# Expert picks of a vision tower's expert layer: one-hot products and sums moved to GpSimd, packing deferred by one tile

## What is computed

```python
q = (hidden_states @ w_queries.T).reshape(b, t, 2, h, n)
sim = jnp.einsum('btphn,hkpn->pbthk', q, keys)
sx, ix = jax.lax.top_k(sim[0], k)
sy, iy = jax.lax.top_k(sim[1], k)
all_scores = (sx[..., :, None] + sy[..., None, :]).reshape(b, t, h, k * k)
all_idx = (ix[..., :, None] * nk + iy[..., None, :]).reshape(b, t, h, k * k)
scores, pos = jax.lax.top_k(all_scores, k)
indices = jnp.take_along_axis(all_idx, pos, axis=-1)
de = down_embed[indices]
ue = up_embed[indices]
ew = jnp.einsum('btd,bthkd->bthk', hidden_states, de)
ew = jax.nn.silu(ew) * jax.nn.softmax(scores, axis=-1)
experts_states = jnp.einsum('bthk,bthkd->btd', ew, ue)
mlp = jax.nn.silu(hidden_states @ w_gate.T) * (hidden_states @ w_up.T) @ w_down.T
return mlp + experts_states
```

## Time and profile before

| | us |
|---|---|
| median of 3 runs (lowest, highest) | 275.31 (274.69, 276.77) |
| profiled execution, its time | 276.26 |
| profiled execution, span of the core | 274.5 |
| TensorE busy | 246.7 (90%) |
| VectorE busy | 181.0 (66%) |
| ScalarE busy | 56.9 (21%) |
| GpSimd busy | 47.7 (17%) |
| chain that ended last | TensorE 50%, VectorE 40% of the span |

### The profile page before, as it was taken

One profiled execution on the slowest core, in us unless ns is written; L12 is line 12 of the kernel. 1 busy time (PEld: TensorE's weight loads), 2 busy tenths in 40 slices (PEclk: granted clock), 3 DMA queues, 4 the chain that ended last, 5 costly groups with the idle time before them and its releaser, 6 DMA issues.

```text
span 274.5 us, 4828 instructions
## 1 busy us (share of the span) xinstructions
PE 246.7 (90%) x1956; PEld 204.2 (74%) x1956; DVE 181.0 (66%) x461; ACT 56.9 (21%) x104; POOL 47.7 (17%) x65
## 2 busy tenths in 40 slices
PE   3998975788865999899999989899979999999996
PEld 2675654677642588889898989888868888888763
DVE  0047298888885139999999999799968767511100
ACT  1101136343453142213131743100000000000000
POOL 5023155001112523224052630000000000000000
PEclk9999999999965699999999999999999999999999
DMA  7960000221003252053115330300000000000000
GB/s 256 383 229 0 2 0 0 89 73 32 19 20 93 58 184 73 0 171 99 39 45 188 111 121 1 88 2 2 0 19 2 0 19 2 0 19 2 19 0 12
DMA packets 14805, 16.99 MB, mean 62 GB/s; under 512 B 848, under 2 KB 12992, under 8 KB 14784
## 3 DMA queue, kind: packets, MB, share of 16 engines
q1 hardware_dynamic: 13776, 15.70, 17.6%
q10 hardware_dynamic: 1008, 1.00, 1.1%
HBM read 15.48 MB, written 1.21 MB: 61 GB/s over the span
## 4 chain that ended last, share of the span: by engine, by line
PE 50%; DVE 40%; issue 3%; ACT 2%; DMA 1%; POOL 1%; DVEq 0%; ACTq 0%
PE ps L1053 20%; PE ps L1016 9%; PE ps L808 7%; PE ps L1075 4%; DVE big L783 4%; DVE topi L684 3%; DVE late L669 3%; PE ps L972 3%; DVE top L681 3%; DVE big L533 2%; PE ps L1050 2%; DVE red L575 2%; DVE big L577 2%; PE ps L835 2%; DVE slots L665 2%
## 5 line engine op out<-in xcount | busy, mean ns | idle before, releaser
L1053 PE MATMUL ps<-ue,big 128*128 128x256 f32 (+1 forms) x320 | 72.3, 381 | 1.4 <-DVE big L783 1.4
L1053 PEld LDWEIGHTS ps<-ue,big 128*128 128x128 f32 (+1 forms) x320 | 57.2, 182 | 12.1 <-DVE big L783 1.8
L1016 PE MATMUL ps<-hn_hi,de_hi 128*128 128x296 f32 x128 | 40.7, 318 | 2.1 <-ACT big L468 1.1
L783 DVE TENSOR_TENSOR big<-ps,big 128x1024 f32<-128x1024 f32 (+1 forms) x19 | 22.7, 1197 | 26.9 <-PE ps L1075 26.2
L1016 PE MATMUL ps<-hn_lo,de_hi 128*128 128x296 f32 x128 | 38.3, 300 | 0.0
L1016 PE MATMUL ps<-hn_hi,de_lo 128*128 128x296 f32 x128 | 38.2, 298 | 0.0
L468 ACT ACTIVATE big<-ps 128x592 f32<-128x592 f32 x32 | 21.1, 666 | 44.5 <-PE ps L1016 44.4
L1016 PEld LDWEIGHTS ps<-hn_hi,de_hi 128*128 128x128 f32 x128 | 24.1, 188 | 4.5 <-DVE actT L730 1.9
L1016 PEld LDWEIGHTS ps<-hn_lo,de_hi 128*128 128x128 f32 x128 | 24.1, 188 | 1.2 <-issue 1.2
L1016 PEld LDWEIGHTS ps<-hn_hi,de_lo 128*128 128x128 f32 x128 | 24.1, 188 | 0.0
L669 DVE TENSOR_TENSOR late<-eqx,wsel 128x2048 f16<-128x2048 f16 (+1 forms) x19 | 22.7, 1197 | 0.7
(11 more groups left out here) (113 smaller groups left out, 337.6 us busy)
## 6 DMA issues: line engine op xcount, KB each, us to landing
de<-in_down_t SPq DMA_DIRECT2D x16, 256.0 KB, 2.8
ue<-in_up_e SPq DMA_DIRECT2D x4, 1024.0 KB, 5.7
big<-in_patches SPq DMA_DIRECT2D x6, 296.0 KB, 5.0
big<-in_w_tok ACTq DMA_DIRECT2D x6, 128.0 KB, 5.3
big<-in_w_qkv SPq DMA_DIRECT2D x1, 768.0 KB, 8.4
h_scratch<-big SPq DMA_DIRECT2D x5, 111.0 KB
late<-in_keys_bd SPq DMA_DIRECT2D x1, 512.0 KB, 9.7
downT<-in_wdown_t SPq DMA_DIRECT2D x1, 512.0 KB, 9.3
```

The lines of the kernel that those rows point to most:

```text
L783: chain(nc.vector.tensor_tensor(dst, pv, dst, ALU.mult), g_ready)
L1016: last = mm(ps[:, 2 + 2 * (e % 2) + a, 0:HALF], half[:, (e // 2) % SPLITS, k, own], src[:, k, a * HALF:(a + 1) * HALF], start=(n == 0), st ...
L1053: last = mm(acc, sil[:, e, j * 128:j * 128 + Q * v], ue[:, e, :], start=False, stop=(e == EX - 1))
```

## The change

VectorE still makes the one-hots of both sides, now into one buffer `oneh` of 128 x 2 x 256 that lies in `xn`, and gives `oneh_ready`. The product with `topf` and the sum over eight, now as three halvings, are done by GpSimd for both sides at once (`picks`). The picks of tile 0 to 3 stand ahead of splits 8, 10, 12 and 14, those of tile 4 behind split 15. `topf` and `pick` have two buffers. The one-hots of tile j wait for the picks of tile j - 1 (`picked`), and the clamp and packing of tile j - 1 (`packed`) stand behind the one-hots of tile j; those of the last tile stand ahead of the denominators.

```diff
+PICK_FROM = 8
...
-        topf = sb("topf", [128, 2, FH, TOPK])
+        topf = sb("topf", [128, 2, 2, FH, TOPK])
...
-        pick = sb("pick", [128, 2, FH, TOPK])
-        oneh = sb("oneh", [128, FH, TOPK, TOPK])
+        pick = sb("pick", [128, 2, 2, FH, TOPK])
...
+        oneh = xn[:, :, :].rearrange("p a (h k c) -> p a h k c", h=FH, k=TOPK)
...
+            def picks(j):
+
+                pool.wait_ge(oneh_ready, 2 * (j + 1))
+                nc.gpsimd.tensor_tensor(oneh[:, :, :, :, :], oneh[:, :, :, :, :],
+                                        topf[:, j % 2].unsqueeze(3).broadcast_to([128, 2, FH, TOPK, TOPK]),
+                                        ALU.mult).then_inc(pick_chain, 1)
+                pool.wait_ge(pick_chain, 3 * j + 1)
+                nc.gpsimd.tensor_tensor(oneh[:, :, :, :, 0:4], oneh[:, :, :, :, 0:4], oneh[:, :, :, :, 4:8],
+                                        ALU.add).then_inc(pick_chain, 1)
+                pool.wait_ge(pick_chain, 3 * j + 2)
+                nc.gpsimd.tensor_tensor(oneh[:, :, :, :, 0:2], oneh[:, :, :, :, 0:2], oneh[:, :, :, :, 2:4],
+                                        ALU.add).then_inc(pick_chain, 1)
+                pool.wait_ge(pick_chain, 3 * j + 3)
+                nc.gpsimd.tensor_tensor(pick[:, j % 2], oneh[:, :, :, :, 0], oneh[:, :, :, :, 1],
+                                        ALU.add).then_inc(picked, 1)
+
             for i in range(EX // 2):
+                if i >= PICK_FROM and (i - PICK_FROM) % 2 == 0:
+                    picks((i - PICK_FROM) // 2)
...
+            picks(TILES - 1)
...
+            def packed(j):
+
+                at = pick[:, j % 2]
+                behind()
+                chain(nc.vector.tensor_scalar(over[:, :, :], at[:, 0], float(EX), float(NK - 1), ALU.is_ge, ALU.mult))
+                chain(nc.vector.tensor_scalar(pack[:, j, 0, :].rearrange("p (h k) -> p h k", h=FH), at[:, 0],
+                                              float(EX - 1), None, ALU.min))
+                behind()
+                chain(nc.vector.tensor_tensor(pack[:, j, 1, :].rearrange("p (h k) -> p h k", h=FH), at[:, 1],
+                                              over[:, :, :], ALU.max))
+
...
                 chain(nc.vector.tensor_copy(self_[:, :, :, :], sel[:, :, :, :]))
+                behind()
+                if j >= 1:
+                    dve.wait_ge(picked, j)
                 for p in range(2):
-                    behind()
-                    chain(nc.vector.tensor_tensor(oneh[:, :, :, :],
-                                                  self_[:, p].unsqueeze(3).broadcast_to([128, FH, TOPK, TOPK]),
+                    chain(nc.vector.tensor_tensor(oneh[:, p], self_[:, p].unsqueeze(3).broadcast_to([128, FH, TOPK, TOPK]),
                                                   iota8.unsqueeze(1).unsqueeze(1).broadcast_to([128, FH, TOPK, TOPK]),
-                                                  ALU.is_equal))
-                    behind()
-                    chain(nc.vector.tensor_tensor(oneh[:, :, :, :], oneh[:, :, :, :],
-                                                  topf[:, p].unsqueeze(2).broadcast_to([128, FH, TOPK, TOPK]),
-                                                  ALU.mult))
-                    behind()
-                    chain(nc.vector.tensor_reduce(pick[:, p], oneh[:, :, :, :], AX.X, ALU.add))
...
+                                                  ALU.is_equal), oneh_ready)
+                if j >= 1:
+                    packed(j - 1)
...
+            dve.wait_ge(picked, TILES)
+            packed(TILES - 1)
             dve.wait_ge(lg_exp, 1)
```

More of the change, by code:

```diff
@@ L250, in vit_tower @@
         split_ready = sem("split_ready")
+        oneh_ready, picked, pick_chain = sem("oneh_ready"), sem("picked"), sem("pick_chain")
         pe_s, sil_ready = sem("pe_s"), sem("sil_ready")
@@ L686, in _ @@
                 behind()
-                chain(nc.vector.tensor_copy(topf[:, :, :, :], topi[:, :, :, :]))
+                chain(nc.vector.tensor_copy(topf[:, j % 2], topi[:, :, :, :]))
                 chain(nc.vector.tensor_tensor(cand[:, :, :, :],
```

## The result

The changed kernel takes 282.69 us (median of 4 runs, 282.12 to 283.3), the kernel before 275.66 beside it; the ratio is 1.0258, with a 95% interval of 1.0221 to 1.0296. It is 7.0 us slower; 283.4 us in all and 8.1 us more had been predicted.

What follows compares the result with a forecast made beforehand. VectorE was taken to set the rounds of 11.87 us, with TensorE alone needing 11.64. Rounds 1.4, last tile 5.6 and clock 1.1 made 8.1 us on the median of 275.3: 283.4 us, range 279.2 to 288.

Steps and rivals of the forecast that it cites:

- The place in the queue: On GpSimd, picks stand behind splits 7, 9, 11, 13, 15, which TensorE holds back, so VectorE waits for them.
- The cost of the picks: Four GpSimd operations per tile, sized by a straight line between two trace rows, with hand-overs: 3.2 us.
- The rounds: Rounds of 12.63 us instead of 11.87, as VectorE's comparison waits for GpSimd's picks; 1.4 us later after three.
- P: Length of one tile's picks on GpSimd, set at 3.2 us, with bounds of 2.42 and 4.8.
- X: Moment in a round when TensorE's odd expert, the second after a gated block, may start, once `actT` frees its banks.
- A sign that came out otherwise: Expected in the profile after: VectorE idle about 2.5 us before the comparison of tiles 1 to 4, released by GpSimd.
- The last tile: Last picks wait for split 15, so VectorE's packing starts 6.85 us later, 1.22 of it idle now: 5.6 us.
- X3: The odd expert's start on TensorE three rounds after the first: 147.46 us before the change, forecast at 148.87.
- The clock: TensorE idles 4.7 us before the first product, its clock falls, and two later rounds no longer fit: 1.1 us.
- The sum: Whole kernel: +1.4 + 5.6 + 1.1 = 8.1 us on the median of 275.3, giving 283.4 us.
- the rival on the other side: Last tile's picks ready in time and not waited for, rounds at TensorE's 11.64 us: faster, 273.8 us; chance 0.04.

Runs made afterwards that it cites:

- both_early: Changed kernel with picks of tiles 0 to 3 ahead of splits 7, 9, 11, 13 and the last tile's ahead of split 14; 277.13 us, ratio 1.006.
- gap_filled: Changed kernel with 28 matmuls that nobody reads added in TensorE's gap behind the second round of slots; 280.68 us, ratio 1.0222.
- load_without_waits: Kernel before, picks still on VectorE, plus the same four operations per tile on GpSimd over scratch, not waited for until long done; 282.57 us.
- longer_picks: Changed kernel with one more product of 128x512 into scratch in each tile's picks on GpSimd; 289.4 us, ratio 1.0534.
- last_on_dve_mid_early: Changed kernel with picks of tiles 0 to 3 one split earlier and the last tile's products and sums back on VectorE; 276.1 us, ratio 1.0038.
- mid_early: Changed kernel with only the picks of tiles 0 to 3 moved one split earlier, the last ones staying behind split 15; 280.57 us, ratio 1.0179.

## Why the prediction was right

**The place in the queue.** It said that VectorE would wait behind splits 7, 9, 11, 13 and 15. It does, at each of the five places, and moving the picks out from behind them takes back 6.3 of 6.65 us in the profiled execution of both_early, 2.0 of 2.6% in whole runs.

**The cost of the picks.** 3.2 us were set, 2.94 to 2.98 measured: 1.28, 0.73, 0.40 and 0.30 us and three hand-overs. The straight line between the earlier trace rows gave 1.29, 0.76, 0.49 and 0.36; the small ones were set too high, and rows of four, two and one neighbouring elements cost nothing above the line. The slope between the two largest is 2.15 ns per element (0.55 us for 256), and 0.12 to 0.18 us per instruction come on top. The Trainium skill, GPSIMD Engine Reference, section on elementwise cycle accounting, has 2.6 cycles at 1.2 GHz for one element; the 2.17 ns worked out from it, an estimate, agree with the slope.

**The rounds.** 1.4 us later at the last `actT` were set, 0.43 measured, under a third. The three rounds use the picks' length each, and the 0.22 to 0.26 us by which P was too high make 0.74 of the difference. The rest is mainly that the picks start 7.14 to 7.25 us behind X and not 7.30. From the end of the picks to the next X it is 2.14 us, as set (2.13), and the first X came where it was set, at 111.33, which is 110.98 without the 0.35 that lie ahead of the first `sims`. The term is a small difference of larger numbers: a round gets longer only from P = 2.44 up.

**A sign that came out otherwise.** VectorE was to be idle for about 2.5 us ahead of the comparison and waited 0.91 from the second wait on. It came to the comparison later than X + 7.9: the cast ahead of it ended at 132.97, X + 9.4, since a rank and this cast, held by GpSimd, took 1.20 and 0.70 us instead of 0.18 and 0.20. The wait hid these holds, so the sum didn't suffer. That is luck, since the prediction had no term for them.

**The last tile.** 5.6 us were set, 5.04 measured: 0.3 because the last picks were done at X3 + 18.1 and not 18.4 (P, mostly), and 0.3 behind the packing. There splits 14 and 15 no longer run beside VectorE: the difference of weights that gives `pack` its last row took 0.62 us before and 0.33 after.

**The clock.** 1.1 us were set. 0.99 were measured in the products' stretch, and gap_filled takes 1.00 of them back there. The 0.19 us behind the stretch are not the clock's: gap_filled keeps 0.15 of them, and what they are is open. The idle time was set at 4.7 us and was 4.73.

**The sum.** Counted from the first `sims` it is 6.65 us where 8.1 were set: every term was set too high, the rounds by 1.0, the last tile by 0.6, the clock by 0.1, and for the 0.19 it had no term. The forecast of 283.4 lies closer to the median of 282.69 than this: the 0.35 us ahead of the first `sims`, and a kernel before that ran at 275.66 beside the new one and not at the 275.3 it was added to, happened to make up half of it.

**What it lacked.** It priced GpSimd's work only through its waits and had no term for what it does to VectorE while it runs. In the changed kernel this hardly shows, since VectorE is waiting for the picks anyway while they run; the cast at 118.67, 1.17 us instead of 0.20, lies ahead of a wait of 1.72. But the rival on the other side was priced by the same omission: with the last picks ready before X3 + 12.8 it promised 273.8 us, 173.6 from the first `sims`. both_early, built to be that kernel, has them ready at X3 + 13.1 (157.52; X3, 3.34 behind its `sims` at 141.07, is 144.41) and needs 175.46. They were late because they waited 1.14 us for the one-hots of a held VectorE, not in GpSimd's queue, and behind the packing's start 2.1 us more of holds follow. Once the waits are gone, the holds take the gain.

## What to carry to other kernels

An engine with little busy time is still a queue: before work is handed to it, look at what stands ahead in its program order and who releases that, and put the work where the queue is free. Work given to GpSimd isn't free for VectorE even then, where both read the on-chip memory: here 4 operations per tile cost VectorE 1.2 us a round (load_without_waits), of the 1.84 that handing them over saves it, without any wait. Fewer and wider instructions on the same engine gave more than the move did at its best.

## What was not expected of the hardware

**The clock can fall after short gaps, and the length of the gap doesn't decide it.** Idle gaps of 1.93 us (longer_picks), 2.28 us and 2.72 us (last_on_dve_mid_early) were followed by a fall. Gaps of 2.25 and 1.89 us later in the same execution of longer_picks, and of 2.75 us in both_early, were not. The same gap of 2.28 us ahead of the change, at about 77.8 us, is in every kernel, and what follows it differs. The table of time of the kernel before, and the same stretch of mid_early's profiled execution:

```profile
78.00:88.00 10.00, 6.92 (x84) 3.73 (x76) 6.68 (x15) 4.37 (x13) 2.26 (x5) 0.50 0.16 48
```

```profile
78.00:88.00 10.00, 4.65 (x82) 2.65 (x68) 7.46 (x17) 4.60 (x15) 2.22 (x5) 0.81 0.25 74
```

The mean clock is 0.50 in the one and 0.81 in the other, TensorE needs 6.92 and 4.65 us for almost the same matmuls (84 and 82 records), and the first `sims` come at 99.39 and 97.19. None of the edits touches this stretch. What decides when the clock falls there is open; no run was made on it. Whole runs of one kernel spread over 2 to 3.4 us here (274.25 to 277.6 for last_on_dve_mid_early), and the spread goes with the mean granted clock: of 17 executions of the kernel before, the one at 0.987 took 273.73 us, eleven at 0.975 274.57 to 275.66 and five at 0.969 276.27 to 276.69. So differences under 1% had to be read from a common point in the trace, or between executions of equal clock.

**One operation held, one operation long.** A held VectorE instruction mostly lasted as long as the rest of the GpSimd operation beside it, about 1.3 us at the most, whatever its own size: 32 elements (L736 in both_early, 1.28 us) as much as 64 (the cast in last_on_dve_mid_early, 1.27). Small instructions lose most by it.
